# Attention and mixture-of-experts layer on one core: the low halves of the expert weights move from a ScalarE pass and a GpSimd subtraction to one VectorE operation

## The reference, cut to what matters

```python
x = x + attn(layernorm(x))      # x: 4 sequences x 512 tokens x 512
x = x + ffn(layernorm(x))
# attn: q, k, v = x @ w_qkv; rope; layernorm of q and k in each of 16 heads of 32
a = jnp.einsum('bhnd,bhmd->bhnm', q, k) ** 4        # fourth power in place of a softmax
a = jnp.tril(a)                                      # causal
out = jnp.einsum('bhnm,bhmd->bhnd', a / a.sum(-1, keepdims=True), v) @ w_out
# ffn: a gate picks 4 of 16 experts for each token; every expert (and a shared one) is
y = jax.nn.silu(x @ g.T) * (x @ u.T) @ d.T           # g, u: 256 x 512, d: 512 x 256
```

## Time and profile before

| | |
|---|---|
| median of 3 runs | 1254.78 us (1251.38 to 1257.58) |
| span of the profiled execution | 1278.8 us |
| busy in it | PE 1013.0, DVE 782.5, ACT 571.1, POOL 503.3 us |
| mean granted TensorE clock | 0.883 of full speed |
| attention loops of sequences 0, 1, 2, 3 | 77.7 to 154.7, 230.9 to 323.9, 397.4 to 490.4, 563.5 to 656.0 us |
| second part | from 684 us on |

### The profile page before, as it was taken

How to read it: one execution, slowest core, us unless ns; L and a number is a source line. 1 busy time by engine, 2 the same in 40 slices (tenths; PEclk the granted TensorE clock), 3 DMA queues, 4 the chain that set the end, 5 groups by cost and what they waited for, 6 DMA issues and landing times. The chain is left out here.

```text
span 1278.8 us, 21813 instructions
## 1 busy us (share of the span) xinstructions
PE 1013.0 (79%) x5786; PEld 483.4 (38%) x5787; DVE 782.5 (61%) x1641; ACT 571.1 (45%) x1018; POOL 503.3 (39%) x738
## 2 busy tenths in 40 slices
PE   5956799666997669976588889888888888878893
PEld 2422245222444214442145445344344344434341
DVE  2855578587695885858955866444544545544442
ACT  2377624767147672366735324333333333323330
POOL 0047500556003751026631102555555555555552
PEclk9977898677996689967787889999999999989997
DMA  8015430144501438104445786777877778877774
GB/s 323 1 50 188 159 131 1 50 149 146 183 3 49 140 107 327 69 0 148 148 149 178 264 321 216 188 171 178 187 185 179 170 177 191 192 154 183 169 178 77
DMA packets 76782, 194.36 MB, mean 152 GB/s; under 512 B 9920, under 2 KB 11072, under 8 KB 75328
## 3 DMA queue, kind: packets, MB, share of 16 engines
q1 hardware_dynamic: 58816, 150.58, 34.5%
q0 software_dynamic: 17920, 43.26, 18.9%
HBM read 132.72 MB, written 61.10 MB: 152 GB/s over the span
## 5 line engine op out<-in xcount | busy, mean ns | idle before, releaser
L606 PE MATMUL bank<-arena,xgT 128*128 (+1 forms) x1152 | 287.4, 387 | 4.0 <-ACT xgT L817 3.1
L853 POOL TENSOR_TENSOR s_p<-s_p,c_causal 128x128 f32<-128x128 f32 x256 | 128.8, 530 | 400.0 <-DVE s_p L1193 397.6
L552 PE MATMUL bank<-s_p,vtok 128*32 128x128 f32 (+3 forms) x512 | 118.0, 605 | 95.9 <-DVE arena L1143 49.5
L810 ACT ACTIVATE hT<-bank 128x512 f16<-128x512 f16 x96 | 57.3, 597 | 276.5 <-PE bank L616 264.6
L462 PE MATMUL bank<-arena 128*128 128x512 f32 x384 | 168.6, 597 | 2.0 <-issue 2.0
L606 PEld LDWEIGHTS bank<-arena,xgT 128*128 128x128 f16 x1152 | 109.6, 100 | 133.5 <-issue 44.4
L627 PE MATMUL bank<-wd,hT 128*128 128x512 f16 x576 | 152.7, 405 | 0.7 <-ACT hT L810 0.7
L898 POOL DMA_INDIRECT out<-yy,sidx x80 | 128.4, 1605 | 45.7 <-issue 44.7
L861 POOL TENSOR_TENSOR arena<-arena 128x768 f16<-128x768 f32 x68 | 115.7, 1702 | 71.9 <-ACT arena L684 71.5
L817 ACT ACTIVATE xgT<-bank 128x1024 f16<-128x1024 f16 x96 | 98.2, 1023 | 90.7 <-PE bank L597 89.1
L1367 DVE TENSOR_SCALAR yy<-bank,hsc 128x512 f32<-128x512 f32 x80 | 60.0, 750 | 125.8 <-DMA out<-yy,sidx 106.6
(11 more groups left out here) (155 smaller groups left out, 1453.3 us busy)
## 6 DMA issues: line engine op xcount, KB each, us to landing
wd<-w_scratch SPq DMA_DIRECT2D x82, 512.0 KB
arena<-w_experts SPq DMA_DIRECT2D x34, 768.0 KB, 5.9
w_scratch<-arena SPq DMA_DIRECT2D x34, 768.0 KB, 4.5
arena<-w_scratch SPq DMA_DIRECT2D x17, 1024.0 KB, 8.0
xin<-x SPq DMA_DIRECT2D x5, 1024.0 KB, 9.1
arena<-x SPq DMA_DIRECT2D x4, 1024.0 KB, 7.1
x_scratch<-arena SPq DMA_DIRECT2D x4, 1024.0 KB, 4.5
xn_scratch<-vtok SPq DMA_DIRECT2D x4, 1024.0 KB, 5.0
```

The lines of the kernel that those rows point to most:

```text
L552: mm = pe.matmul(bank[6 + n][r, P * kb:N], w, s_p4[:, (i - 1) % 2, j, 0:N - P * kb], start=(kb == 0), stop=(kb == MB - 1), skip_group_chec ...
L606: mm = pe.matmul(bank[2 + k][:], xgT[:, k, xh * EC + c, :], w, start=(c == 0 and xh + wh == 0), stop=(c == EC - 1 and xh == 1))
L853: pool.tensor_tensor(d, d, C["causal"][:], ALU.mult).then_inc(p4_masked, 1)
```

## The change

The low half is made by one DVE operation from the unscaled number: `stage` x 256 minus the high half. ACT's second pass and the semaphore between the two passes are gone, and POOL has only its masks left in the loop. DVE does the low half of step i - 1 in step i, behind its two fourth powers and ahead of everything else in that step (`finish` too); the one of step 15 comes behind the last `finish`. In the second part it comes behind `hidden(t)` for t = 0 to 3.

```diff
-                act.activation(halves[:, j, 0, a], stage[:, j, a], ACT.Copy, scale=WS).then_inc(high_written, 1)
-                act.wait_ge(high_written, n)
-                act.activation(stage[:, j, a], stage[:, j, a], ACT.Copy, scale=WS).then_inc(hi_done, 1)
+                act.activation(halves[:, j, 0, a], stage[:, j, a], ACT.Copy, scale=WS).then_inc(hi_done, 1)
...
-                    split_lo(b, i)
-
-            def split_lo(b, i):
-
-                j, q = i // 2 % 2, i % 2
-                a = slice(q * PIECE, q * PIECE + PIECE)
-                pool.wait_ge(hi_done, b * (NG * MB) + (i + 1))
-                pool.tensor_tensor(halves[:, j, 1, a], stage[:, j, a], halves[:, j, 0, a], ALU.subtract
-                                   ).then_inc(lo_done, 1)
...
-            for i in range(4):
-                split_lo(B, i)
...
+            def split_lo(b, i):
+
+                j, q = i // 2 % 2, i % 2
+                a = slice(q * PIECE, q * PIECE + PIECE)
+                dve.wait_ge(hi_done, b * (NG * MB) + (i + 1))
+                dve.scalar_tensor_tensor(out=halves[:, j, 1, a], in0=stage[:, j, a], scalar=WS, in1=halves[:, j, 0, a],
+                                         op0=ALU.mult, op1=ALU.subtract).then_inc(lo_done, 1)
...
                         dve.tensor_tensor(s_p4[:, i % 2, j, 0:N - P * kb], s2, s2, ALU.mult).then_inc(p4_done[0], 1)
+                    if i:
+                        split_lo(b, i - 1)
                     if i and kb == 0:
                         finish(b, i // MB - 1)
...
                 finish(b, NG - 1)
+                split_lo(b, NG * MB - 1)
...
                 b = B - 1
+                if t < 4:
+                    split_lo(B, t)
                 if t == 0:
                     compare(mb[:], NX)
```

More of the change, by code:

```diff
@@ L252, in build @@
         v_sb, qkT_ps, qkT_sb = sem("v_sb"), sem("qkT_ps"), sem("qkT_sb")
-        qk_lo, high_written, norm_known, logits_sb = map(sem, ("qk_lo", "high_written", "norm_known", "logits_sb"))
+        qk_lo, norm_known, logits_sb = map(sem, ("qk_lo", "norm_known", "logits_sb"))
         p4_done = [sem("p4_done_even"), sem("p4_done_odd")]
@@ L677, in _, with split_hi @@
             act.wait_ge(memset_done, 1)
-            def split_hi(j, q, n):
+            def split_hi(j, q):
                 a = slice(q * PIECE, q * PIECE + PIECE)
-                act.activation(halves[:, j, 0, a], stage[:, j, a], ACT.Copy, scale=WS).then_inc(high_written, 1)
-                act.wait_ge(high_written, n)
-                act.activation(stage[:, j, a], stage[:, j, a], ACT.Copy, scale=WS).then_inc(hi_done, 1)
+                act.activation(halves[:, j, 0, a], stage[:, j, a], ACT.Copy, scale=WS).then_inc(hi_done, 1)
             def split_next(b, i):
@@ L692, in split_next @@
                         act.wait_ge(halves_out[j], b * (16 * MB) + 16 * (i // 4))
-                split_hi(j, q, b * (NG * MB) + (i + 1))
+                split_hi(j, q)
             def copy_rows(b, m):
```

## The result

Measured alternately with the kernel before, the changed kernel took 1264.87 us (median of 11 runs, 1258.23 to 1270.01) against 1260.06 us (11 runs): ratio 1.0062, interval 1.0037 to 1.0087, so 8 us slower (5 to 11). The ratio is not the quotient of these two medians, which is 1.0038 and lies at the lower end of the interval. In a second study the ratio was 1.0057 (1.0025 to 1.0089), and that of its medians 1.0060. The prediction was 4 us slower (1259 on a base of 1254.78, ratio 1.0033) with a range up to 1.011.

A forecast was written before the change was run, and what follows sets the result against it. No engine was seen as always busy: sequence 0 follows an ACT-DVE-PE chain, sequences 1 to 3 mostly wait for DVE. Terms 0 + 5.7 - 1.5 gave +4.2 us, so 1259 from 1254.78; range 1247 to 1269.

The forecast's parts named there:

- slower rival: In sequences 1 to 3 each low half waits for a mask: about 20 us slower, less 1.5, 1273 us; chance 0.25.
- Price of the low half: DVE's new 768-column operation takes 0.95 us, 0.87 on DVE's path, and 1.2 where it lets a mask through.
- The stalls that go: DVE's stalls beside POOL's low half vanish: 7.8 us in each of sequences 1 to 3, about 1.2 in a sequence 0 finish.
- The masks are held: In the loop, DVE's low half delays POOL's remaining masks, then PE's products and the scores; bounds 0 and 0.87 us.
- masks not held: Rival: the low half lets masks pass; sequence 0 gains 5 us, the others lose 1.0 each; 1251 us, chance 0.12.
- Sequence 0: Attention loop of sequence 0: 0.2 us gained per group, 0.5 at the start, losses at the end; sum about 0.
- Sequences 1 to 3: Attention loops of sequences 1 to 3: low halves and held masks cost 1.9 us each, 5.7 in all.
- second finish late by over 1 us: Sign expected in the loops of sequences 1 to 3, where the second finish was forecast +1.3 us.
- Second part: Start of the second part: four low halves cost DVE 3.5 us, vanished stalls give back 5.0; -1.5 us.
- if ACT waits for a load: Sign that the forecast is wrong: ACT waiting for a weight load, whose delays were forecast to add 0.
- DMA paragraph: Weight loads behind the low half on SP's queue: tightest at step 8 of sequence 0, hidden by ACT's pause; 0.
- ACT's time arrives: Faster rival: sequence 0 gains 7.7 us, sequences 1 to 3 come out even; -9.2 us, 1246, chance 0.13.

## Why the prediction was right or wrong, point by point

**The outcome.** Slower by 4 us was forecast, slower by 8 (5 to 11) was measured. The forecast had no change as the likeliest outcome, at 0.48 against 0.37 for slower by over 0.5%; the measured ratio lies just on the slower side of that limit. The range held it. The slower rival (20 us, each low half paid with a mask in front) was not what happened: the operation did take 1.21 us in most places, but on the path it cost no more than forecast.

**The sum agrees (+4.2 forecast, +4.4 in the trace up to the one-hot rows), its terms do not.** That is luck. The forecast had the loss in the loops of sequences 1 to 3; most of it was in the head of sequence 3, for which it had nothing, and terms of the other sign that it had too small or not at all made up for it.

- *Price of the low half:* 0.95 us alone and 1.2 beside a mask forecast, 0.94 and 1.21 measured. Right.
- *The stalls that go:* right in every line named.
- *The masks are held:* right, and so semaphores are not the only thing that holds one engine back for another, as I had said at the start. With the low half ahead of the fourth powers ACT came to step 8 of sequence 0 0.90 us earlier; the bounds were 0 and 0.87. The 6.1 and 1.5 us that this move gave in sequence 0 and in each other loop hold more than the masks, and can't be set against the 5 and 0.9 of the "masks not held" rival. By the Trainium skill ("SBUF — State Buffer", "SBUF: two separate sides") the pair is locked for a whole instruction and the loser waits; the trace agrees for a scalar-tensor-tensor operation in both roles (1.21 us for it, 1.16 for the one mask that waits for it). "One operation each", as I had it, is not the rule in all places: one mask waited through seven operations of DVE.
- *Sequence 0:* 0 forecast, -1.6 measured. Step 8 came 5.60 us after step 6, not 5.8, and the reciprocal after 9.1, not 9.5. Two masks did get in ahead of the reciprocal, but they cost 0.17 us (the second fourth power took 0.86 against 0.69) and 0.26 (the low half 1.20 against 0.94), 0.43 and not 0.6. The third finish came 2.9 us earlier where 1.1 was forecast; in the group shown, 0.3 us of it are faster scores behind the reciprocal. From there to the last finish 1.3 were lost, with 0.9 forecast.
- *Sequences 1 to 3:* +5.7 forecast in all, +0.2, +1.3 to 1.6 and +1.2 to 1.5 measured, 3 in all. The first finish came 1.1 us earlier and not 0.3: the fourth powers ahead of it took 6.8 us before and 5.6 after, and in these sequences I had counted POOL's stalls in the routing lines alone. In sequences 2 and 3 the later finishes are shifted by this 0.8 and otherwise near the forecast (second finish +0.7 and +0.4, third +0.4 and +0.1). The second finish late by over 1 us, which I had named as a sign, was not seen. In sequence 1 it even came 0.7 us earlier, since the loops of before are not alike: its stretch from the first finish to the second took 24.1 us, that of the others 22.7 to 23.1, in both profiles, and 24.5 in all loops of the changed kernel. I had worked out sequence 1 and multiplied by three.
- *Second part:* -1.5 forecast, -2.9 measured. I had left out what ACT's pass gives there: with that alone gone the stretch is 86.8 instead of 88.8.
- *The loads of the weights:* "if ACT waits for a load" was one of my signs of being wrong, and ACT does, three times in sequence 0, for 1.7 us in all. The DMA paragraph had the load for step 8 come 0.6 us late and the pause of step 10 take it up. ACT waits 0.60 us there, and its pause at step 10 is 3.91 us long. So the sum is not touched, and the sign was too strict.
- *Head of sequence 3:* 0 forecast, +6.8 measured. **This is the step that failed.** The DMA paragraph asked of each half when its load is wanted by ACT, and found 3 us of room. It did not ask what else stands on SP's queue behind the wait for the low half of step 15: the five expert loads. They have no deadline of their own for 200 us, but they move 5 MB, and with 3 us of delay they still kept the DMA engines busy when DVE jumped back to the start of its loop. DVE went on 6.3 us later and not 0.33 (its code came late, by the reading above), PE stood for 3.4 us and then lost 3.1 us at the lower clock. The store of the normed rows was pushed back as well, but nothing in the traces waits for that in the end. Moving those loads on SP's queue alone brought the kernel back to 1.0001.
- *Head of sequence 1:* 78.9 before in both profiles, 77.1 after in both; not forecast. All of it is PE at another granted clock, as the rows show. Half a microsecond is the projection (15.70 us against 15.18, at 0.89 and 0.92), and 1.4 us are the gate's matmuls and the transposes between them (8.35 us against 6.96). PE had paused for 3.0 us before these in both; they ran at 0.50 throughout before, and began at 1.00 after. Why the clock stayed up longer was not tried.

**The rivals.** "ACT's time arrives" (-9 us) comes near to what ACT's pass alone gave (0.9915, 11 us), though the rival was a sum with DVE's low half in it. It failed together with that low half, since that is then what the masks, and PE, wait for. This is the larger error of judgement behind a right sign: I took the two halves of the change as one trade. One is worth 0.85%, the other then costs 1.5%.

**What stays open.** The trace accounts for 4.4 us of a measured 8 (5 to 11). The other 3 lie at the edge of the interval or in the tiles behind, where single executions differ by 14 to 20 us; profiles can't tell. That DVE's wait at the loop's branch is one for its code is argued and not shown, and why it is 2.9 us already where no loads are in the way was not tried. Nor was the cost of the masks that wait through many operations of DVE.

## What to carry to other kernels

When an operation moves to another engine, list what waits for its result in the DMA queue, and then everything that stands in that queue behind this wait, deadline or not: a bulk load that starts 3 us later can keep the DMA engines busy just when somebody needs them, and the reader may be an engine's own code behind a loop's branch. When an engine stands longer, look which wait ended last for the engine that matters: here the long wait of ACT for a store was a bystander. On DVE, put an operation like this low half, with two inputs in SBUF, where POOL has nothing to do, or it holds POOL's short operations, and whatever waits for them, by up to its whole length. And split a change that does two things into its halves before judging it: here one half was worth keeping alone.

## What the runs showed of the hardware

- DVE and POOL mostly take turns at single operations, in both directions: 768 columns on DVE go from 0.94 to 1.21 us beside masks, and four masks from 1.9 to 2.7 us beside one low half. But one mask of 0.45 us also stood for 3.11 us while DVE went through seven operations. An engine's busy time includes this waiting: POOL's masks show 172 us after the change and 129 before, for the same work.
- Five loads of 1 MB issued at 490.5 us doubled the time of a 1 MB store issued 16 us later (9.7 us against 5.0 with the loads issued 20 us ahead of it, 5.1 with them behind it).
- At the branch of a hardware loop DVE went on after 0.33 us in the kernel before, after 2.8 to 3.3 us in the kernels with the low half on DVE, and after 6.2 to 6.4 us where the five loads kept the DMA engines busy.
- A pause of 3.4 us of PE was followed by 5 us at a granted clock of 0.50, and 24 matmuls took 13.4 us instead of 10.5.
- Up to the one-hot rows two executions agree to 0.1%; in the tiles with indirect DMAs they differ by up to 4%.
